# Two attentions joined: norms in halves, weight products and first inputs of the wide attention made in the first attention's last sequences

## The reference, cut to what matters

```python
x = x + _L0_attn_ref(_layernorm(x), ...)             # 16 heads of 8, ALiBi and causal mask
x = x + _L0_xattn_ref(ctx_1024, _layernorm(x), ...)  # the "wide" attention: 16 heads of 64
x = x + _L0_ffn_ref(_layernorm(x), ...)
x = x + _L1_attn_ref(_layernorm(x), ...)
x = x + _L1_xattn_ref(_layernorm(x), ctx_1024, ...)
x = x + _L1_ffn_ref(_layernorm(x), ...)

def _L0_xattn_ref(x, latents, ln1_w, ln1_b, ln2_w, ln2_b, Wq, Wkv, Wo):
    xn = _layernorm(x, ln1_w, ln1_b)            # the context, 77 rows
    latn = _layernorm(latents, ln2_w, ln2_b)    # a second norm on the normed x
    q = latn @ Wq
    k, v = jnp.split(jnp.concatenate([xn, latn], axis=1) @ Wkv, 2, axis=-1)
    # heads(...), softmax(q k^T / 8) v, per head
    return out @ Wo
```

## Time and profile before

| | us |
|---|---|
| median of 3 runs | 2369.62 |
| lowest and highest | 2365.26, 2372.1 |
| the profiled execution | 2365.84 |
| its span in the trace | 2364.0 |
| end of the first attention's last product | 288.58 |
| step 0 of the wide loop | 322.57 |
| one pair in the loop | 42.60 |

### The profile page before, as it was taken

One profiled execution on the slowest core, in us unless ns is written; L12 is line 12 of the kernel. 1 busy time (PEld: TensorE's weight loads), 2 busy tenths in 40 slices (PEclk: granted clock), 3 DMA queues, 4 the chain that ended last, 5 costly groups with the idle time before them and its releaser, 6 DMA issues.

```text
span 2364.0 us, 48963 instructions
## 1 busy us (share of the span) xinstructions
PE 2068.0 (87%) x14977; PEld 1746.3 (74%) x14977; DVE 1677.4 (71%) x3675; ACT 1300.1 (55%) x3026; POOL 921.8 (39%) x981
## 2 busy tenths in 40 slices
PE   5999789999999999981057999988869999999998
PEld 3787579999999999940045788766657777777776
DVE  5666468877777778778974666666557777787775
ACT  2555346666666666655423555655545555555554
POOL 3111044444444444305312111233325666656565
PEclk7999879999999999985577999988869999999999
DMA  5445500000000000000004344444414333433333
GB/s 174 139 126 138 125 1 2 2 1 1 0 1 1 0 1 1 2 0 0 0 5 127 112 124 125 132 136 144 144 54 124 122 123 119 128 116 121 119 122 103
DMA packets 217848, 178.10 MB, mean 75 GB/s; under 512 B 36005, under 2 KB 184549, under 8 KB 217573
## 3 DMA queue, kind: packets, MB, share of 16 engines
q1 hardware_dynamic: 216828, 175.88, 24.8%
q10 hardware_dynamic: 864, 0.43, 0.1%
HBM read 133.77 MB, written 43.15 MB: 75 GB/s over the span
## 4 chain that ended last, share of the span: by engine, by line
PE 53%; issue 17%; POOL 10%; DVE 7%; SPq 6%; DMA 3%; ACT 3%; POOLq 0%; DVEq 0%; ACTq 0%
POOL h_lo L1797 6%; PE bank L229 5%; PE bank L1516 4%; PE bank L1517 4%; PE bank L1518 4%; PE bank L773 4%; PE bank L240 4%; SPq L616 3%; PE bank L737 3%; PE bank L739 3%; PE bank L738 3%; PE bank L211 3%; PE bank L784 3%; PE bank L227 2%; PE bank L210 2%
## 5 line engine op out<-in xcount | busy, mean ns | idle before, releaser
L1797 POOL TENSOR_TENSOR h_lo<-h,h_hi 128x512 fp32r<-128x512 f32 x264 | 341.0, 1292 | 244.5 <-ACT h_hi L1617 244.4
L427 DVE TENSOR_REDUCE nm<-bank 128x4 f32<-128x512 f32 (+1 forms) x384 | 238.3, 621 | 238.4 <-PE bank L211 236.1
L1053 POOL TENSOR_TENSOR pw<-ew,rw 128x410 f32<-128x410 f32 x256 | 225.8, 882 | 379.5 <-DVE rw L963 344.7
L355 ACT ACTIVATE pt<-bank 128x512 f32<-128x512 f32 (+1 forms) x384 | 228.5, 596 | 220.7 <-PE bank L229 216.8
L229 PE MATMUL bank<-q_pack,k_diag 128*128 128x128 f32 (+1 forms) x1536 | 271.3, 303 | 26.0 <-DMA q_pack<-nmt 26.0
L1738 DVE TENSOR_TENSOR bank<-bank,sl 128x512 f32<-128x512 f32 x264 | 184.2, 698 | 149.4 <-PE bank L1518 120.7
L1610 ACT ACTIVATE sl<-bank 128x512 f32<-128x512 f32 x264 | 157.9, 598 | 239.8 <-PE bank L1518 238.4
L876 ACT ACTIVATE ew<-bank,nmax 128x205 f32<-128x205 f32 x512 | 217.0, 432 | 123.0 <-DVE nmax L955 122.9
L229 PEld LDWEIGHTS bank<-q_pack,k_diag 128*128 128x128 f32 (+1 forms) x1536 | 218.3, 190 | 57.7 <-issue 24.3
L773 PE MATMUL bank<-kvt,qs 128*128 128x205 f32 x1024 | 221.6, 339 | 0.8 <-DVE qs L974 0.8
L211 PE MATMUL bank<-k_diag,q_pack 128*128 128x512 f32 (+1 forms) x384 | 210.6, 551 | 0.1
(11 more groups left out here) (280 smaller groups left out, 5430.2 us busy)
## 6 DMA issues: line engine op xcount, KB each, us to landing
share_b<-share_rows SPq DMA_DIRECT2D x256, 256.0 KB, 3.2
q_pack<-q_rows SPq DMA_DIRECT2D x96, 256.0 KB, 3.1
k_diag<-k_rows SPq DMA_DIRECT2D x256, 64.0 KB, 2.7
q_rows<-q_hi SPq DMA_DIRECT2D x96, 128.0 KB, 2.1
k_rows<-k_hi SPq DMA_DIRECT2D x96, 128.0 KB, 2.1
raw<-in_experts SPq DMA_DIRECT2D x33, 192.0 KB, 2.4
q_rows<-q_lo SPq DMA_DIRECT2D x48, 128.0 KB, 2.1
k_rows<-k_lo SPq DMA_DIRECT2D x48, 128.0 KB, 2.1
```

The lines of the kernel that those rows point to most:

```text
L355: nc.scalar.activation(m.pt[0:a.keys, c, :, :].rearrange("p h t -> p (h t)"), m.flip[c % 2][0:a.keys, :], ACT.Exp).then_inc(s.exped.semaph ...
L427: nc.vector.tensor_reduce(m.nm[:, u % 2, :].rearrange("p (h c) -> p c h", c=NC)[:, c, :], m.score[c % 2][:, 0:HC * a.columns].rearrange("p ...
L1053: nc.gpsimd.tensor_tensor(m.pw[:, k, :, 0:KW], m.ew[:, k, :, :], m.rw[:, k, :].unsqueeze(2).broadcast_to([128, 2, KW]), ALU.mult)\
L1797: nc.gpsimd.tensor_tensor(m.h_lo[:, k % 3, :], m.h[:, (k + u) % 2, :], m.h_hi[:, k % 3, :].bitcast(F32), ALU.subtract).then_inc(s.los, 1)
```

## The change

Everything between the two stages moves to other places.

- Norms are made in halves. `variances`, `norms` and the second norm (now `renorm_begin` and `renorm_end`) for sequences 0 to 15 of x and of the context run in the first attention's sequences 24 to 26, for 16 to 31 in steps 5, 8, 10 and 13 of pair 1 of the wide attention. The roots of ScalarE go to sequences 24 and 25 and to steps 5 and 9 of pair 1. The context has temporaries of its own.
- The eight groups of weight products run at c = 1 and c = 3 of sequences 27 to 30, in one bank (bank 7), their high parts at c = 2 and c = 0, their low parts at c = 3 and c = 1.
- The first pair's inputs are normalised in sequence 26, the second's in 30, and the transposes, copies, first queries and first scores lie in 30 and 31 and in the gaps of the last sequence (`in_gap`). Clears of `kv` and `pw` shrink to the parts that no other write covers.
- The four 512 KB loads are issued two in sequence 24 and two in 25, the affine rows in 26, the other 16 loads four each from 27 to 30.
- In the wide loop `normalise(p + 2)` is spread over steps 5, 7, 9 and 11, `statistics` go to 13 and 15, `extremes` (of pair p - 2) to 1 and 3, and GpSimd's inputs to 1, 3, 5, 7 and 10.

```diff
@@ wide_tensor
+    def tail(b, c):
+        if (b, c) == (27, 1):
+            pe.wait_ge(m.s.products_in, m.product_loads)
+            wait(pe, first.keys, B)
+        if 27 <= b <= 30 and c % 2 == 1:
+            weight_products(2 * (b - 27) + c // 2)
+        if (b, c) == (30, 1):
+            pe.wait_ge(m.s.zeros, 5)
+            wait(pe, first.max_s, B)
+            transpose_inputs(0, 0, 0, 0)
+        if (b, c) == (30, 3):
+            pe.wait_ge(s.inputs_t, 1)
+            transpose_inputs(0, 0, 1, 0)
+        if (b, c) == (31, 1):
+            pe.wait_ge(s.inputs_t, 2)
+            ask(0, 0, 0)
+        if (b, c) == (31, 3):
+            scores(0, 0, 0)
+            ask(0, 0, 1)
@@ wide_scalar
+            if isinstance(p, int) and (p, n) == (1, 5):
+                root_scalar(act, nc, m, m.s, 6, at=SECOND)
+                root_scalar(act, nc, m.c, m.s, 7, L, at=SECOND)
+            if isinstance(p, int) and (p, n) == (1, 9):
+                root_scalar(act, nc, m, m.s, 8, at=SECOND)
+    def tail(b, c):
+        if (b, c) == (24, 1):
+            root_scalar(act, nc, m, m.s, 3, at=FIRST)
+            root_scalar(act, nc, m.c, m.s, 4, L, at=FIRST)
+        if (b, c) == (25, 3):
+            root_scalar(act, nc, m, m.s, 5, at=FIRST)
+        if c == 2 and 27 <= b <= 30:
+            weight_highs(2 * (b - 27))
+        if c == 0 and 28 <= b <= 31:
+            weight_highs(2 * (b - 28) + 1)
+        if (b, c) == (30, 2):
+            copy_inputs(0, 0, 0)
+        if (b, c) == (31, 0):
+            copy_inputs(0, 0, 1)
@@ wide_vector
+    def normalise(p, i):
+        k, b = i // 2, 2 * p + i // 2
+        if i == 0:
+            wait(dve, s.latents, 2 * p - 1)
+            wait(dve, s.contexts, 2 * p - 1)
...
+    def rest_of_norms(n):
+        if n == 5:
+            wait(dve, first.measured, B)
+            variances(nc, m, m.s, link, m.stats, at=SECOND)
+            dve.wait_ge(m.s.stats, 2 * B)
+            variances(nc, m.c, m.s, link, m.cstats, L, at=SECOND)
+        elif n == 8:
+            norms(nc, m, m.s, link, 6, m.stats, m.rstd, m.shift, at=SECOND)
+            renorm_begin(nc, m, m.s, link, SECOND)
+        elif n == 10:
+            norms(nc, m.c, m.s, link, 7, m.cstats, m.crstd, m.cshift, L, at=SECOND)
+        elif n == 13:
+            renorm_end(nc, m, m.s, link, 8, SECOND)
...
-            if n == 1 and pair_exists(p + 1):
-                normalise(p + 1)
-            if n in (5, 7) and pair_exists(p - 1):
-                statistics(p - 1, (n - 5) // 2)
-            if n == 11 and pair_exists(p - 1):
-                extremes(p - 1)
+            if n in (5, 7, 9, 11) and pair_exists(p + 2):
+                normalise(p + 2, (n - 5) // 2)
+            if n in (13, 15) and pair_exists(p - 1):
+                statistics(p - 1, (n - 13) // 2)
+            if n in (1, 3) and pair_exists(p - 2):
+                extremes(p - 2, (n - 1) // 2)
...
+            if isinstance(p, int) and p == 1:
+                rest_of_norms(n)
+    def tail(b, c):
+        if (b, c) == (24, 1):
+            wait(dve, first.measured, B // 2)
+            variances(nc, m, m.s, link, m.stats, at=FIRST)
+            dve.wait_ge(m.s.stats, B + B // 2)
+            variances(nc, m.c, m.s, link, m.cstats, L, at=FIRST)
+        if (b, c) == (24, 3):
+            norms(nc, m, m.s, link, 3, m.stats, m.rstd, m.shift, at=FIRST)
+            renorm_begin(nc, m, m.s, link, FIRST)
+        if (b, c) == (25, 3):
+            norms(nc, m.c, m.s, link, 4, m.cstats, m.crstd, m.cshift, L, at=FIRST)
+        if (b, c) == (26, 1):
+            renorm_end(nc, m, m.s, link, 5, FIRST)
+        if (b, c) == (26, 3):
+            wait(dve, first.transposed, B)
+            for i in range(4):
+                normalise(0, i)
+        if c == 3 and 27 <= b <= 30:
+            weight_lows(2 * (b - 27))
+        if c == 1 and 28 <= b <= 31:
+            weight_lows(2 * (b - 28) + 1)
+        if (b, c) == (30, 3):
+            for i in range(4):
+                normalise(1, i)
+        if (b, c) == (31, 3):
+            copy_queries(0, 0, 0)
@@ wide_pool
-            if n in (2, 4, 6, 8, 11) and pair_exists(p + 1):
-                inputs(p + 1, 1 - v, (2, 4, 6, 8, 11).index(n))
+            if n in (1, 3, 5, 7, 10) and pair_exists(p + 1):
+                inputs(p + 1, 1 - v, (1, 3, 5, 7, 10).index(n))
@@ load_more
-                    if b >= B - 2 * SLOTS:
-                        for dst, src in later_loads[3 * (b - B + 2 * SLOTS):3 * (b - B + 2 * SLOTS) + 3]:
+                    if b in (24, 25):
+                        for dst, src in product_loads[2 * (b - 24):2 * (b - 24) + 2]:
+                            sp.dma_start(dst, src).then_inc(m.s.products_in, 16)
+                    if b == 26:
+                        for dst, src in affine_loads:
+                            sp.dma_start(dst, src).then_inc(m.s.affine_in, 16)
+                    if b >= 27:
+                        for dst, src in later_loads[4 * (b - 27):4 * (b - 27) + 4]:
                             sp.dma_start(dst, src).then_inc(m.s.wide_in, 16)
```

More of the change, by code:

```diff
@@ L389, in body @@
                 copy_heads(*before)
+            if tail is not None and isinstance(b, int):
+                tail(b, c)
     if a.earlier is None:
@@ L575, in body @@
             clear_later()
+        if tail is not None and isinstance(b, int):
+            tail(b)
     if a.earlier is None:
@@ L828, in body @@
                 wait(pe, s.updated, p)
+            if n == 3 and isinstance(p, int) and p == 0:
+                pe.wait_ge(first.updated.semaphore, B)
             if n in (8, 10) and pair_exists(p + 1):
```

303 lines of the change are left out of this document (163 added, 140 removed).

## The result

The changed kernel takes 2357.41 us (median of 20 runs, 2351.22 to 2368.32), the kernel before beside it 2365.24 (20 runs): a ratio of 0.9968, 95% interval 0.9953 to 0.9983. It is 7.8 us faster where 28 were forecast, and the time lies outside the range of 2326 to 2355. The profiled execution of the changed kernel took 2354.38 us (span 2352.6), 11.5 less than that of before.

What follows compares the result with a forecast made beforehand. TensorE was taken to bound the wide attention, with a ladder of small steps before it. Terms -33.5, -14.6, -3.5, +12, +1, +9 and +1.5 sum to -28.1 us; forecast 2339 us, range 2326 to 2355.

Steps and rivals of the forecast that it cites:

- The ladder goes, -33.5: Between first attention and wide loop: the stretch of small steps leaves, about 0.5 us remains, 33.5 us saved.
- `kvt_lo`, -14.6: Wide-attention pairs: GpSimd makes kvt_lo one step earlier, so TensorE's wait for it goes, 14.6 us saved.
- Weight loads in two halves, -3.5: First attention's tail: fewer 512 KB loads ahead of the maxima row shorten its wait, 3.5 us saved, between 0 and 9.
- Halved norms, +1: Sequences 24 to 26: first-half norms mostly hide before the wait for the maxima row, costing 1 us, bounds 0 and 4.
- Weight products, 3.8 for the work: Sequences 27 to 30: eight groups of four matmuls at full clock add 3.8 us on TensorE.
- 6.4 for the waits: Sequences 27 to 30: product groups sharing one bank wait for VectorE's low parts, 6.4 us, bounds 4.2 and 9.6.
- Clock, +1.5: End of first attention: one fall of TensorE's clock, lasting into step 1 or 2, costs 1.5 us, bounds 0 and 4.
- Pair 1, +9: Pair 1 of the wide attention: second-half norms on VectorE and ScalarE cost 9 us, nearer the serial 13.4.
- Both, serial insertions and no gain in the loop: Rival for tail, pair 1 and loop: inserted work costs in series and the loop gains nothing; 2364 us, chance 0.04.
- three signs of being wrong: Pairs not shorter; maxima-row wait staying with norms on top; VectorE waiting for `kv` in step 5.
- Slower by waits for `kv`: Rival in step 5 of every pair: VectorE waits until GpSimd has written `kv`; 2381 us at 3 us each, chance 0.04.
- Table switches at twice the row: Rival in pair 1: ScalarE's four table loads cost twice the profile's 1.28 us each; 2344 us, chance 0.03.

## Why the prediction was wrong, point by point

- *The ladder goes, -33.5:* right, -31.6. Between the last output product and step 0 some 2.4 us remain, not 0.5.
- *`kvt_lo`, -14.6:* right as a mechanism (alone -16.6 in the pairs, no wait of line 753 for `kvt_lo` left in the loop). It failed for the changed kernel because the sum had no term for the loop's turn: I took 42.60 for every pair of the loop, though five in the trace of before took 44.1. The change of ScalarE's instruction count was costed at nothing; it gave back 8 us, 2.7 us a turn in place of 1.4 (the middle turns), while ScalarE's code was fetched.
- *Weight loads in two halves, -3.5:* nothing in the sum; 2.9 us were won in sequence 24 and 3.9 lost in the next two, the end at 0 that was named. *Halved norms, +1:* mis-sized, 4.7. The cover named held but for 1.3 us; the cost came in sequences 26 to 28, with a lower clock and a longer wait, for which the term had nothing.
- *Weight products, 3.8 for the work:* the step failed by reading two records as two matmuls; 10.2. *6.4 for the waits:* 5.9 measured. *Clock, +1.5:* bounded at 4, it was in the wrong place; the clock is 0.81 through sequences 26 to 28, where the wait for the row and the waits of the groups follow on each other. Busy time over the nine sequences is 7.3 us less where it doesn't fall.
- *Pair 1, +9:* mis-sized, 12.5. The nearness to the serial bound of 13.4 hides two errors that work against each other: VectorE's blocks last 11.3 us and not 7.6, and not all of the series is seen.
- The rival *Both, serial insertions and no gain in the loop* (2364, 0.04) came nearest in its mechanisms, but the loop's gain was not absent: it was made and given back at a place that no rival named. *Slower by waits for `kv`* did not come: no such wait is in pair 2 to 13. *Table switches at twice the row* fell: leaving out four loads gave 4.1 us, and four times 1.28 are 5.1; by the Trainium skill's 2.66 (ScalarE: Activation LUTs, What ACT_TABLE_LOAD costs) it would have been 10.6, an estimate from the page's figure.

Of what the next profile was to show, the pairs of 41.6 and the missing wait came; step 0 near 298, the 12 to 14 us, 2 to 3 us a sequence and pair 1 near 50 did not: 310, 13.35 one sequence earlier, 5 to 7 us in sequences 27 and 28, and 55. Of the three signs of being wrong, two did not come. The third came in part: a wait of 3.35 us for the row of maxima stayed, and the norms cost 4.7 us.

## What to carry to other kernels

An edit that adds or removes instructions ahead of a loop moves that loop in its engine's code. Here that made a turn of it up to 2.7 us dearer or cheaper. Compare pairs with and without a turn, and look at the packets of the instruction queues and their times, before a gain or a loss is given to the edit itself. Work can hide where it stands and be paid for three sequences later, so leave it out once and compare stretch by stretch, not the sum alone. A duration read in one place need not hold in another: linked operations of 0.21 us took up to 0.98 beside GpSimd's. Count records per instruction before multiplying a duration. And a sum that comes out near the measured value is no proof of its terms.

## What the runs showed of the hardware that was not expected

- ScalarE's loop cost 0 to 3.0 us at each turn (middle turns) by the place of its code. Where it cost anything, five packets of 8 KB went over an instruction queue in each round, three of them at the turn; where it cost nothing, none did. The first packet starts with ScalarE's stand, and the stand ends 1.6 to 1.9 us after it (kernel before) or 1.4 to 1.7 us after the second one (changed kernel). The cost was the same when the code lay 128 instructions further.
- The profile can name a wait for another engine there: ScalarE's 9.2 us of stands behind TensorE's line 739 in the kernel before were gone once ScalarE's own code was moved.
- Six small operations of VectorE in pair 1 took 0.65 to 0.98 us in place of 0.17 to 0.23, each until 0.03 to 0.04 us after an operation of GpSimd beside it had ended.
- Four table loads left out gave 4.1 us (2.6 to 5.4); their rows are of 1.28 us each, and one lay beside VectorE's work.
- Open: where in the code the borders lie that make one fetch or two hold up the turn, how the norms bring the lower clock of sequences 26 to 28, and the 15 us by which the work after the last `pw` differs between kernels whose code there differs only in place.
